# A fused graph-attention, linear-attention and expert layer on one core: the scatter of each expert slot's result is moved behind the slot's own values

## The chip, the core and the metric

The kernel runs on one core of a Trainium2 chip. A core has TensorE (PE in the profile, with its weight loads as PEld), VectorE (DVE), ScalarE (ACT), GpSimd (POOL) and SyncE (SP), which here only issues transfers, and 16 DMA engines which they share. The engines run on their own and wait for each other through semaphores. The metric is the time of one execution on the device, in microseconds (us), as the median of several runs.

## What is computed

```python
xn = _layernorm(x)                                  # x: 384 tokens x 1024
x = x + gnn(xn, edges) + mix(xn)                    # graph attention and linear attention
x = x + ffn(_layernorm(x))                          # the experts

def ffn(xt):                                        # 32 experts, each 1024 x 512 and 512 x 1024
    gates = sigmoid(xt @ expert_sel.T)
    sel_val, sel_idx = top_k(gates, 4)              # four experts for each token
    gate_full = zeros.at[arange(N)[:, None], sel_idx].set(sel_val)
    scores = relu(einsum('nd,edf->nef', xt, keys)) * gate_full[:, :, None]
    return einsum('nef,efv->nv', scores, values)
```

All data are float32. The change touches only the last line's stage, the experts.

## The kernel before

The first 474 us of the profiled execution are the two attention branches and the routing. The rest is the expert stage, which is computed in **slots**. A slot is a batch of 128 lanes (64 tokens for each of two experts, side by side); there are 16 such whole slots, 0 to 15, for the 32 experts, and behind them at least one shared slot of four experts with 32 lanes each, which takes the tokens that did not fit. Its experts are the four whose weights are still in memory from slots 14 and 15; with this input one shared slot runs.

For one slot s the work is, in the order of its data:

- `gather` (POOL, L716): an indirect transfer fetches the rows of the slot's 128 tokens into the one buffer `etmp`. It is issued when the transposes of the slot before have read the buffer.
- `x_T(s)` (PE, L1668): eight transposes of these rows into two banks of the matmul memory (PSUM); ACT (L877) and DVE (L1272) copy one half each to `xgT`.
- `do_keys(s)` (PE, L1585): 32 matmuls, two experts side by side on two halves of the array, into bank 0. ACT (L884) applies relu and gate into `hsb`.
- `h_T(s)` (PE, L1676): four transposes of `hsb` into bank 1; ACT (L888) copies them to `hT`.
- `do_values(s, v)` for v = 0, 1 (PE, L1585): 16 matmuls each, into banks 4 and 5. ACT (L894, `y_hi`) takes the rounded high part `yh`, then DVE (L1279, `y_lo`) the remainder `yl`.
- `put_block(s)` (PE, L1625 and L1626): the scatter. A one-hot matrix `place` (DVE, L1275) times `yh` and `yl` puts the lanes back to the 384 tokens: six puts g = 0 to 5 of two matmuls each, g = 0 to 2 for the columns of v = 0 and g = 3 to 5 for those of v = 1, into banks 6, 7, 4, 5, 6, 7.
- `y_add(s, g)` (DVE, L1284): six additions into the accumulator `acc`.

The waits inside `put_block` matter here: put 0 waits for `yl` of v = 0, put 3 for `yl` of v = 1, and puts 4 and 5, which use banks 6 and 7 for the second time, wait for the additions of puts 0 and 1 of the same slot. Nothing sets the order but the program text: each engine runs its own list, written out by hand. On PE one pass for slot s is `do_keys(s+1)`, `put_block(s-1)`, `x_T(s+2)`, `h_T(s+1)`, `do_values(s)`; so a slot's scatter stands behind the keys of the slot after next. Only the end differs: `put_block(14)` stands directly between the values of slot 14 and those of slot 15, since there are no further keys there.

The weights come from HBM in chunks of 1 MB, eight for a slot (four of keys, four of values), into a ring of 18 places. SP issues a chunk when PE has used up the pair of chunks that held its place before (semaphore `s_spent`, L578 for the middle slots, L623 for keys of slot 15 and values of slots 14 and 15).

Of the kernel before, what the change touches and what calls it, by code (L numbers as in the profile page):

```python
# [37 lines left out]
WHOLE = NE // 2  # L38
# [72 lines left out]
def gps_layer_kernel(nc, x, edges, etw, W, cols, rows, selT, keys, values, C, xt_dram, out):  # L111
# [3 lines left out]
    with ctx:  # L115
# [107 lines left out]
        biv_b = at("biv_b", [P, D], F32, BIV)  # L223

        call = sb("c_all", [P, sum(w for _, w in CONSTS_AT)], F32)
        cst, width = {}, 0
        for n, w in CONSTS_AT:
# [318 lines left out]
        def keys_at(s):  # L546
            return 8 * s - 4 if s >= 2 else 8 * s

        def values_at(s):
            return 8 * s + 8 if s == 1 or 2 <= s < WHOLE - 1 else 4 if s == 0 else 8 * WHOLE - 4  # L550
# [386 lines left out]
        def _(dve):  # L937
# [332 lines left out]
            def x_evict(s, p):  # L1270
                dve.wait_ge(s_xT, s)
                nc.vector.tensor_copy(xgT[p][:, 4:8, :], x_halves[1]).then_inc(s_xd, 1)  # L1272

            def place_of(s, p):
                nc.vector.tensor_scalar(place[p][:, :], iota[:, :], tokf[:, bass.ds(s, 1)], None, ALU.is_equal).then_inc(s_place, 1)  # L1275

            def y_lo(s, v):
                dve.wait_ge(s_yh, 2 * s + v + 1)
                nc.vector.tensor_tensor(yl[:, v, :], ps[4 + v], yh[:, v, :].bitcast(F32), ALU.subtract).then_inc(s_yl, 1)  # L1279

            def y_add(s, g, bank):
                dve.wait_ge(s_put, 6 * s + g + 1)
                rows_of = acc[:, g % NT, g // NT * HALF:(g // NT + 1) * HALF]
                nc.vector.tensor_tensor(rows_of, ps[bank], rows_of, ALU.add).then_inc(s_add, 1)  # L1284

            def dve_slot(s, p, x_ahead=True):
                for g in range(6):
                    y_add(s - 1, g, put_banks[g])
                if x_ahead:
                    x_evict(s + 2, p)  # L1290
                place_of(s, p)
                for v in range(2):
                    y_lo(s, v)
# [4 lines left out]
            y_lo(0, 0)  # L1298
            x_evict(1, 1)
            y_lo(0, 1)  # L1300
            x_evict(2, 0)
            dve_slot(1, 1)
            with dve.Fori(1, WHOLE // 2 - 1) as j:
                for p in range(2):
                    dve_slot(2 * j + p, p)
            dve_slot(WHOLE - 2, 0)
            dve_slot(WHOLE - 1, 0, x_ahead=False)
            turns = dve.value_load(slots[0:1, 0:1], min_val=1, max_val=TURNS_MAX)
# [12 lines left out]
        def _(pe):  # L1321
# [55 lines left out]
            for name in order:  # L1377
# [52 lines left out]
                elif name == "o1":  # L1430

                    for b in range(NT):
                        bs = slice(b * P, (b + 1) * P)
                        for q in range(4):
                            s = j["sub"] + q
# [10 lines left out]
                else:  # L1446
                    xh, xl = src_of[base]
                    for q in range(4):
                        s = j["sub"] + q
# [109 lines left out]
            def token_table():  # L1559

                for q in range(NT * TOPK):
                    if q % TOPK == 0:
                        pe.wait_ge(s_1s, q // TOPK + 1)
                        pe.wait_ge(s_1h, q // TOPK + 1)
                    last = nc.tensor.matmul(ps[5][:, 0:SLOTS], lane1h_h[:, q, :], slot1h_h[:, q // TOPK, q % TOPK, :],
                                            start=(q == 0), stop=(q == NT * TOPK - 1))
                last.then_inc(s_r, 1)
# [11 lines left out]
            def two_experts(c, to, what, k, kc, first, fin):  # L1579

                for side in range(2):
                    half = slice(LANES * side, LANES * side + LANES)
                    if kc == 0:
                        pe.wait_ge(s_ring[at_place[c + side]], ring_landed(c + side, 0))
                    last = nc.tensor.matmul(to[half, :], what[:, k, half], ring[at_place[c + side]][:, kc, :], start=first, stop=fin)  # L1585
                if kc == 3:
                    last.then_inc(s_spent, 1)
# [29 lines left out]
            def put(s, g, p, bank):  # L1617

                v, t = g // NT, g % NT
                if g == 0:  # L1620
                    pe.wait_ge(s_place, s + 1)
                if t == 0:
                    pe.wait_ge(s_yl, 2 * s + v + 1)
                to = place[p][:, t * P:(t + 1) * P]
                nc.tensor.matmul(ps[bank], to, yh[:, v, :], start=True, stop=False)  # L1625
                nc.tensor.matmul(ps[bank], to, yl[:, v, :], start=False, stop=True).then_inc(s_put, 1)  # L1626

            def put_block(s, p, where=put_banks):

                for g in range(6):  # L1630
                    if g in (0, 1) and (not isinstance(s, int) or s >= 1):
                        pe.wait_ge(s_add, 6 * s - 1 + g)
                    if g >= 4:
                        pe.wait_ge(s_add, 6 * s - 3 + g)
                    put(s, g, p, where[g])

            def do_keys(s, p):

                if isinstance(s, int) and s == 0:
                    pe.wait_ge(s_xa, 1)  # L1640
                else:
                    pe.wait_ge(s_xa, s + 2)
                    pe.wait_ge(s_h, s)
                for k in range(DC):
                    if k == DC // 2:
                        if isinstance(s, int) and s == 0:
                            pe.wait_ge(s_xa, 2)
                        else:
                            pe.wait_ge(s_xd, s)
                    if k == TABLE_AT and isinstance(s, int) and s == 0:  # L1650
                        token_table()
                    two_experts(keys_at(s) + 2 * (k // 4), ps[0], xgT[p], k, k % 4, k == 0, k == DC - 1)

            def do_values(s, p, v):
                if v == 0:
                    pe.wait_ge(s_he, s + 1)
                if not isinstance(s, int) or s >= 1:
                    pe.wait_ge(s_add, 6 * s - 3 + v)
                for k in range(EF):
                    two_experts(values_at(s) + 2 * v, ps[4 + v], hT[p], k, k, k == 0, k == EF - 1)  # L1660

            def x_T(s, p, landed):
                pe.wait_ge(s_g[p], landed)
                pe.wait_ge(s_xa, s + 1)
                if not isinstance(s, int) or s >= 2:
                    pe.wait_ge(s_xd, s - 1)
                for b in range(DC):
                    last = nc.tensor.transpose(ps[2 + b // 4][:, (b % 4) * P:(b % 4 + 1) * P], xg[:, b * P:(b + 1) * P], ident[:, :])  # L1668
                last.then_inc(s_xT, 1)

            def h_T(s):
                pe.wait_ge(s_h, s + 1)
                if not isinstance(s, int) or s >= 1:
                    pe.wait_ge(s_he, s)
                for b in range(EF):
                    last = nc.tensor.transpose(ps[1][:, b * P:(b + 1) * P], hsb[:, b * P:(b + 1) * P], ident[:, :])  # L1676
                last.then_inc(s_hT, 1)

            def pe_slot(s, p):

                do_keys(s + 1, 1 - p)
                put_block(s - 1, 1 - p)
                x_T(s + 2, p, 16 * ((s + 3) // 2))
                h_T(s + 1)
                for v in range(2):
                    do_values(s, p, v)

            do_keys(0, 0)
            gate_table()
# [1 line left out]
            do_values(0, 0, 0)  # L1691
            x_T(1, 1, 16)
            do_values(0, 0, 1)
            do_keys(1, 1)
            x_T(2, 0, 16)
            h_T(1)
            for s in range(1, WHOLE - 1):
                pe_slot(s, s % 2)
            put_block(WHOLE - 2, 0)
            for v in range(2):  # L1700
                do_values(WHOLE - 1, 1, v)
            pe.wait_ge(s_slots, 1)
# [57 lines left out]
```

## Time and profile before

| | |
|---|---|
| median of 3 runs | 804.27 us (804.12 to 805.77) |
| the profiled execution | 806.2 us, its span 804.4 us |
| mean granted TensorE clock | 0.998 of full speed |
| busy: PE / PEld / DVE / ACT / POOL | 779.8 / 546.2 / 401.2 / 245.5 / 200.6 us |
| transferred | 207.10 MB, 257 GB/s over the span |
| chain that ended last | PE 79%, SP's queue 6%, DMA 5%, DVE 5% |

The profile cuts the span into 40 slices. From the 26th on (502 us) the rate of the transfers stands at 422 to 427 GB/s in each slice until the 38th (764 us), and the DMA engines are busy without a gap. The busy digit of PE stands at 9 in the same slices, and at 8 in the last of them. Two resources are thus full at once in the expert stage, and the share of busy time alone does not say which of them sets the end.

### The profile page before, as it was taken

The numbers are of one execution on the slowest core, as the hardware profiler recorded it, in microseconds if no ns is written. First come the engines' busy times: TensorE is split into PE (matmuls) and PEld (weight loads), VectorE is DVE, ScalarE is ACT, GpSimd is POOL, SyncE is SP. The second block draws the span as 40 slices with busy tenths as digits, with TensorE's granted clock in tenths as the row PEclk, the third lists the DMA queues.
The fourth block names the chain that finished last, engine by engine and source line by source line (L and its number), as shares of the span: only waits on it lengthen the run. The fifth ranks groups of instructions, "written<-read, shape, count | busy, mean of one in ns | idle before, by whom it ended". The sixth has DMA issues, their size and how long they took to land.

```text
span 804.4 us, 11580 instructions
## 1 busy us (share of the span) xinstructions
PE 779.8 (97%) x4187; PEld 546.2 (68%) x4187; DVE 401.2 (50%) x892; ACT 245.5 (31%) x426; POOL 200.6 (25%) x213
## 2 busy tenths in 40 slices
PE   6999999999999999999999999999999999999897
PEld 6997889988998999997557754444444444444333
DVE  6579976753443346436873784232233323322234
ACT  4453421342332234337882231211111211111101
POOL 2027434544534440006890001100000010000000
PEclk9999999999999999999999999999999999999999
DMA  8962534243343434431107889999999999999936
GB/s 341 404 238 84 204 140 158 59 145 112 115 149 105 143 120 170 151 105 53 53 2 282 346 348 377 425 425 422 427 425 426 426 425 426 425 426 425 424 116 252
DMA packets 35606, 207.10 MB, mean 257 GB/s; under 512 B 7812, under 2 KB 8196, under 8 KB 12256
## 3 DMA queue, kind: packets, MB, share of 16 engines
q1 hardware_dynamic: 27504, 190.85, 59.5%
q0 software_dynamic: 7184, 14.71, 4.9%
q10 hardware_dynamic: 864, 0.83, 0.3%
q8 instruction: 33, 0.54, 0.3%
q14 instruction: 21, 0.17, 0.1%
HBM read 204.91 MB, written 4.43 MB: 260 GB/s over the span
## 4 chain that ended last, share of the span: by engine, by line
PE 79%; SPq 6%; DMA 5%; DVE 5%; issue 2%; ACT 1%; POOL 1%; DVEq 0%; POOLq 0%; ACTq 0%
PE ps L1585 20%; PE ps L1324 14%; PE ps L1326 14%; PE ps L1325 14%; SPq L578 5%; DMA raw<-in_keys 3%; PE ps L1625 2%; PE ps L1626 2%; PE ps L493 2%; PE ps L1597 2%; PE ps L1668 1%; PE ps L482 1%; PE ps L467 1%; DMA etmp<-xt_dram,gidx 1%; SPq L623 1%
## 5 line engine op out<-in xcount | busy, mean ns | idle before, releaser
L965 DVE TENSOR_TENSOR wl<-raw,wh 128x1024 fp32r<-128x1024 f32 x88 | 108.3, 1235 | 118.3 <-ACT wh L771 117.7
L771 ACT ACTIVATE wh<-raw 128x1024 fp32r<-128x1024 f32 x88 | 93.0, 1060 | 193.6 <-PE ps L1326 192.5
L698 POOL DMA_INDIRECT plane<-code,idx x96 | 101.9, 1061 | 120.7 <-DMA plane<-code,idx 95.4
L1284 DVE TENSOR_TENSOR acc<-ps,acc 128x512 f32<-128x512 f32 x102 | 62.5, 681 | 102.8 <-PE ps L1626 102.8
L1585 PE MATMUL ps<-ring,xgT 128*64 128x512 f32 x376 | 100.8, 593 | 3.4 <-DMA ring<-in_keys 3.4
L1585 PE MATMUL ps<-ring,hT 128*64 128x512 f32 x424 | 103.4, 596 | 0.7 <-ACT hT L888 0.7
L1324 PE MATMUL ps<-xnh,wh 128*128 128x384 f32 x256 | 86.9, 340 | 0.9 <-DVE xnl L1059 0.9
L1326 PE MATMUL ps<-xnh,wl 128*128 128x384 f32 x256 | 86.5, 338 | 0.0
L1325 PE MATMUL ps<-xnl,wh 128*128 128x384 f32 x256 | 86.5, 338 | 0.0
L1279 DVE TENSOR_TENSOR yl<-ps,yh 128x512 fp32r<-128x512 f32 x34 | 23.5, 691 | 99.8 <-ACT yh L894 99.8
L1585 PEld LDWEIGHTS ps<-ring,xgT 128*64 128x64 f32 x376 | 31.4, 137 | 58.6 <-issue 52.4
L1585 PEld LDWEIGHTS ps<-ring,hT 128*64 128x64 f32 x424 | 32.4, 137 | 54.0 <-issue 52.2
L456 POOL TENSOR_SCALAR pr<-pr,mx 128x384 f32<-128x384 f32 x40 | 49.4, 1253 | 69.6 <-DVE mx L419 69.6
L714 POOL COPY gcol<-gidx 128x1 int32 (+1 forms) x16 | 2.9, 183 | 244.1 <-PE ps L1668 244.1
L894 ACT ACTIVATE yh<-ps 128x512 fp32r<-128x512 f32 x34 | 20.3, 598 | 103.0 <-PE ps L1585 97.1
L1324 PEld LDWEIGHTS ps<-xnh,wh 128*128 128x128 f32 x256 | 48.1, 188 | 1.3 <-DVE xnl L1059 1.2
L1585 PE MATMUL ps<-raw,xgT 128*64 128x512 f32 x136 | 47.5, 595 | 1.4 <-DMA raw<-in_keys 1.2
L1325 PEld LDWEIGHTS ps<-xnl,wh 128*128 128x128 f32 x256 | 48.1, 188 | 0.1
L1326 PEld LDWEIGHTS ps<-xnh,wl 128*128 128x128 f32 x256 | 48.1, 188 | 0.0
L884 ACT ACTIVATE hsb<-ps,tabf 128x512 f32<-128x512 f32 x16 | 11.0, 689 | 110.4 <-PE ps L1585 103.8
L1625 PE MATMUL ps<-yh,place 128*128 128x512 f32 x102 | 42.4, 416 | 0.0
L1626 PE MATMUL ps<-yl,place 128*128 128x512 f32 x102 | 40.1, 393 | 0.0
(258 smaller groups left out, 1396.6 us busy)
## 6 DMA issues: line engine op xcount, KB each, us to landing
ring<-in_values SPq DMA_DIRECT2D x53, 1024.0 KB, 23.3
ring<-in_keys SPq DMA_DIRECT2D x49, 1024.0 KB, 21.8
raw<-in_keys SPq DMA_DIRECT2D x19, 1024.0 KB, 18.1
raw<-in_values SPq DMA_DIRECT2D x11, 1024.0 KB, 25.7
raw<-in_w_v SPq DMA_DIRECT2D x8, 1024.0 KB, 4.9
raw<-in_w_q SPq DMA_DIRECT2D x8, 1024.0 KB, 4.8
raw<-in_w_k SPq DMA_DIRECT2D x8, 1024.0 KB, 4.8
key_rows<-key_dram POOLq DMA_DIRECT2D x6, 1024.0 KB, 5.8
```

The lines of the kernel that those rows point to most:

```text
L456: nc.gpsimd.tensor_scalar(pr[:, u % RING, :], pr[:, u % RING, :], mx[:, 3, u:u + 1], None, ALU.mult).then_inc(s_p, 1)
L578: sp.dma_start(ring[at_place[n]], src_ap[bass.ds(e[side], 1), half].rearrange("a p k n -> p (a k) n"))\
L698: nc.gpsimd.indirect_dma_start(plane[m], bass.IndirectOffsetOnAxis(idx[:, g:g + 1].bitcast(U32), 0), code[:, g:g + 1], None, bounds_check= ...
L771: nc.scalar.activation(wh[:, s % SUB], raw[:, c % RAW, 2 * (s % 2):2 * (s % 2) + 2, :], ACT.Copy)\
L965: nc.vector.tensor_tensor(wl[:, s % SUB], raw[:, (s // 2) % RAW, 2 * (s % 2):2 * (s % 2) + 2, :], wh[:, s % SUB].bitcast(F32), ALU.subtrac ...
L1284: nc.vector.tensor_tensor(rows_of, ps[bank], rows_of, ALU.add).then_inc(s_add, 1)
L1324: nc.tensor.matmul(o, ah, bh_, start=start, stop=False)
L1325: nc.tensor.matmul(o, ah, bl_, start=False, stop=False)
L1326: return nc.tensor.matmul(o, al, bh_, start=False, stop=stop)
L1585: last = nc.tensor.matmul(to[half, :], what[:, k, half], ring[at_place[c + side]][:, kc, :], start=first, stop=fin)
L1625: nc.tensor.matmul(ps[bank], to, yh[:, v, :], start=True, stop=False)
L1626: nc.tensor.matmul(ps[bank], to, yl[:, v, :], start=False, stop=True).then_inc(s_put, 1)
```

## The change

PE's program is written in another order: `put_block(s)` follows directly on `do_values(s)`, for all slots 0 to 13 (for slot 14 it already does), in place of standing behind `do_keys(s+2)`. On DVE the copy of the rows for slot 2 (`x_evict(2, 0)`) moves behind the six additions of slot 0. ACT, POOL and SP have the instructions that they had, in the same order, and no instruction is added or removed.

```diff
@@ vector @@
             def dve_slot(s, p, x_ahead=True):
                 for g in range(6):
                     y_add(s - 1, g, put_banks[g])
+                if isinstance(s, int) and s == 1:
+                    x_evict(2, 0)
                 if x_ahead:
                     x_evict(s + 2, p)
...
             y_lo(0, 1)
-            x_evict(2, 0)
             dve_slot(1, 1)
@@ tensor @@
             def pe_slot(s, p):
                 do_keys(s + 1, 1 - p)
-                put_block(s - 1, 1 - p)
                 x_T(s + 2, p, 16 * ((s + 3) // 2))
                 h_T(s + 1)
                 for v in range(2):
                     do_values(s, p, v)
+                put_block(s, p)
...
             do_values(0, 0, 1)
+            put_block(0, 0)
             do_keys(1, 1)
             x_T(2, 0, 16)
             h_T(1)
             for s in range(1, WHOLE - 1):
                 pe_slot(s, s % 2)
-            put_block(WHOLE - 2, 0)
             for v in range(2):
                 do_values(WHOLE - 1, 1, v)
```

On PE at slot 1, before. The `xgT0` rows are keys of slot 2, `yh_97,place0_99` with `yl` the scatter of slot 0, `etmp` and `hsb` the transposes `x_T(3)` and `h_T(2)`, `hT1` the values of slot 1, and `ring2_79,xgT1_94` the first keys of slot 3:

```order
L1585 MATMUL ps<-ring15_90,xgT0_93 64x512
L1625 MATMUL ps<-yh_97,place0_99 128x512
L1626 MATMUL ps<-yl_98,place0_99 128x512
...
L1668 MATMUL ps<-c_all,etmp 128x128 x8
L1676 MATMUL ps<-c_all,hsb_101 128x128 x4
L1585 MATMUL ps<-ring16_91,hT1_96 64x512
...
L1585 MATMUL ps<-raw_76,hT1_96 64x512 x8
L1585 MATMUL ps<-ring2_79,xgT1_94 64x512
```

The same stretch after the change (line numbers are one higher):

```order
L1586 MATMUL ps<-ring15_90,xgT0_93 64x512
L1669 MATMUL ps<-c_all,etmp 128x128 x8
L1677 MATMUL ps<-c_all,hsb_101 128x128 x4
L1586 MATMUL ps<-ring16_91,hT1_96 64x512
...
L1586 MATMUL ps<-raw_76,hT1_96 64x512 x8
L1626 MATMUL ps<-yh_97,place1_100 128x512
L1627 MATMUL ps<-yl_98,place1_100 128x512
...
L1586 MATMUL ps<-ring2_79,xgT1_94 64x512
```

The twelve matmuls of a scatter have gone from between the keys and the transposes, and those of the slot's own result (`place1`, slot 1) stand between its values and the next keys.

On DVE at the first slots, as a difference. `xgT_93` is the copy of the rows for slot 2, `xgT_94` that for slot 1 and then for slot 3:

```order
 L1279 TENSOR_TENSOR yl<-ps,yh 128x512
+L1284 TENSOR_TENSOR acc<-ps,acc 128x512 x6
 L1272 COPY xgT_93<-ps 128x512
-L1284 TENSOR_TENSOR acc<-ps,acc 128x512 x6
 L1272 COPY xgT_94<-ps 128x512
```

The six additions of slot 0 now come ahead of the copy for slot 2, as their puts do on PE.

## Rows read from the trace of the kernel before

**Rows 1.** Windows: length, busy us by engine, granted clock, DMA share, GB/s

```profile
547.38:565.54 18.16, 18.16 (x91) 8.03 (x89) 5.99 (x10) 2.97 (x5) 1.25 (x2) 1.00 1.01 423
...
768.00:780.00 12.00, 12.00 (x68) 4.04 (x71) 5.52 (x10) 1.19 (x2) 0.00 (x0) 1.00 0.05 20
```

**Rows 2.** Waits of PE after 503 us: waiter, releaser, us in total, times, longest

```profile
PE ps L1585 <- DMA ring<-in_keys: 3.4, 3, 1.3
...
PE ps L1585 <- DMA raw<-in_keys: 1.2, 1, 1.2
```

**Rows 3.** Chain that ended last, from 700 us: start, length, what

```profile
723.90 27.96 DMA raw<-in_keys
751.90 3.65 PE ps L1585 x14
```

**Rows 4.** Timeline of PE: last keys, scatter, transposes, values, as in every slot

```profile
546.86 0.59 PE L1585 MATMUL ps<-ring,xgT 128*64 128x512 f32 x1
547.38 0.50 PE L1625 MATMUL ps<-yh,place 128*128 128x512 f32 x1
...
550.25 1.03 PE L1668 MATMUL ps<-c_all,etmp 128*128 128x128 f32 x8
551.12 0.60 PE L1676 MATMUL ps<-c_all,hsb 128*128 128x128 f32 x4
551.65 0.65 PE L1585 MATMUL ps<-ring,hT 128*64 128x512 f32 x2
```

**Rows 5.** Timeline of PE, then ACT, where no scatter stands between keys and transposes

```profile
501.76 0.59 PE L1585 MATMUL ps<-raw,xgT 128*64 128x512 f32 x1
502.28 1.09 PE L1668 MATMUL ps<-c_all,etmp 128*128 128x128 f32 x8
503.21 0.64 PE L1676 MATMUL ps<-c_all,hsb 128*128 128x128 f32 x4
...
502.46 0.69 ACT L884 ACTIVATE hsb<-ps,tabf 128x512 f32<-128x512 f32 x1 [6.33 <-PE ps L1585]
```

**Rows 6.** Timeline of PE, ACT, DVE: scatter of slot 14, directly behind its values

```profile
765.82 1.03 PE L1585 MATMUL ps<-ring,hT 128*64 128x512 f32 x4
766.78 0.50 PE L1625 MATMUL ps<-yh,place 128*128 128x512 f32 x1
...
768.27 0.50 PE L1625 MATMUL ps<-yh,place 128*128 128x512 f32 x1
...
769.81 0.40 PE L1626 MATMUL ps<-yl,place 128*128 128x512 f32 x1
770.13 1.08 PE L1585 MATMUL ps<-ring,hT 128*64 128x512 f32 x4
...
766.90 0.60 ACT L894 ACTIVATE yh<-ps 128x512 fp32r<-128x512 f32 x1 [2.84 <-PE ps L1585]
...
767.53 0.69 DVE L1279 TENSOR_TENSOR yl<-ps,yh 128x512 fp32r<-128x512 f32 x1 [2.75 <-ACT yh L894]
768.14 3.67 DVE L1284 TENSOR_TENSOR acc<-ps,acc 128x512 f32<-128x512 f32 x6
```

**Rows 7.** Two gathers on L716: start, and us from issue to landing

```profile
L716 POOL DMA_INDIRECT etmp<-xt_dram,gcol x1: 1043/1043/1043, 493.2 to 493.2; - x1
...
DMA to landing us min/median/max: 4.9/4.9/4.9
...
L716 POOL DMA_INDIRECT etmp<-xt_dram,gcol x1: 1017/1017/1017, 504.7 to 504.7; - x1
...
DMA to landing us min/median/max: 8.9/8.9/8.9
```

**Rows 8.** Timeline of PE: first transpose of the rows of slot 3

```profile
513.93 1.04 PE L1668 MATMUL ps<-c_all,etmp 128*128 128x128 f32 x8
```

**Rows 9.** L623, two of the value chunks: duration and start of issues, us to landing

```profile
L623 SPq DMA_DIRECT2D ring<-in_values x2: 333/3595/6857, 733.1 to 733.7; - x2
DMA to landing us min/median/max: 28.5/29.4/30.3
```

## The prediction

> **What bounds the kernel now.** I read the page first, for the stage: from 502 us to 764 us both PE and the DMA engines are full. Busy shares can't rank them, so the next view is the windows. A middle slot takes 18.16 us with PE busy for all of it while the transfers run at 423 GB/s [rows 1]. A slot's eight chunks and its gather are 8.4 + 0.5 = 8.9 MB, which at that rate take about 21 us. PE uses weights faster than they arrive; it lives on the ring, which was full when the stage began. The waits show when that store runs out: after 503 us PE waits for weights four times, 3.4 + 1.2 = 4.6 us in all [rows 2], and all of it late, in the keys of slots 13, 14 and 15 (the rows do not name the slots; their place follows from the last wait, below, one slot of about 21 us apart). The last wait ends at 751.90 us, where the chain that ended last goes over from a transfer of 27.96 us to PE [rows 3]. Behind it nothing more is waited for from HBM, and from 768 to 780 us PE is full with the DMA engines at 0.05 [rows 1]. So the end is set by the weights, **but only by 4.6 us**: had PE needed 4.6 us more of its own before 751.9 us, those waits would be gone and the end would be where it is. What the change is worth depends on how much PE time it adds, against that reserve.
>
> **What the change does to PE in one slot.** The same twelve matmuls run, so only the joints between pieces differ.
>
> Where the scatter is taken out: before, from the last keys pair to the first values matmul it is 551.65 - 546.86 = 4.79 us [rows 4]. After, it is keys, `x_T`, `h_T`, values. The trace has that sequence once, since slot 1's keys have no scatter behind them: last pair to `x_T` 502.28 - 501.76 = 0.52 us, `x_T` to `h_T` 503.21 - 502.28 = 0.93 us [rows 5]. The latter has a new wait in it: `h_T` needs `hsb`, which ACT finishes at 502.46 + 0.69 = 503.15 us [rows 5]; the scatter used to cover that. It is small, since eight transposes without a wait take 551.12 - 550.25 = 0.87 us [rows 4]. From `h_T` to values 0.53 us [rows 4]; `hT` of that slot is a slot old by then, so nothing waits. Sum 0.52 + 0.93 + 0.53 = 1.98 us, against 4.79: **2.81 us less**.
>
> Where it is put in: the trace has this once too, at slot 14 [rows 6]. The first put starts at 766.78, the next work at 770.13: 3.35 us. The same block in the middle takes 550.25 - 547.38 = 2.87 us [rows 4]. The chain inside is plain: values end, `yh` at 766.90 for 0.60 us, `yl` at 767.53 for 0.69 us, and put 3, which needs this `yl`, starts at 768.27. The first six matmuls just about cover it. Then DVE's additions, 3.67 / 6 = 0.61 us each from 768.14 us, pace puts 4 and 5, because banks 6 and 7 must be read before they are written again. Before the change the additions were paced by PE, now PE by the additions. To that comes the joint from values to scatter: the last group of values is two pairs of matmuls from 765.82 on, 1.03 us with the 0.59 of one matmul [rows 4], so pairs follow each other after some 0.43 us; the last pair starts at 766.25 and the put 0.53 us later, where the next keys pair would follow after 0.43 us: 0.10 us. Put in: 3.35 + 0.10 = **3.45 us more**.
>
> Net 3.45 - 2.81 = **0.64 us for each moved scatter**. Fourteen are moved (slots 0 to 13): 14 x 0.64 = 9.0 us. The row that could be too pessimistic is the last joint, 770.13 - 769.81 = 0.32 us from the last put matmul to the values [rows 6], where a put matmul in the middle of the stage takes 2.87 / 12 = 0.24; it might be a wait for an addition that keys don't have. Without it the term is 14 x 0.54 = 7.6 us. I take 8.7, near the measured pair, and keep 7.6 and 9.0 as ends. Queued behind the waiting puts on PE are the next keys, and behind them SP's issues, which wait for used chunks; those come later by the same time.
>
> **The gather of slot 3.** In the prologue keys 1 and keys 2 follow each other with no values between, so the two `x_T` there lie closest. Before, `x_T(2)` starts at 502.28 and `x_T(3)` at 513.93 [rows 5, 8], with the scatter of slot 0 between; the gather for slot 3 is issued at 504.7 and lands 8.9 us later, at 513.6 [rows 7], 0.3 us ahead of need. Now the scatter of slot 0 stands ahead of keys 1: `x_T(2)` and the gather's issue move by 3.45 us, to 505.7 and 508.1; `x_T(3)` would be ready at 513.93 + 3.45 - 2.87 = 514.5. With 8.9 us the gather lands at 517.0 and PE waits 2.5 us; with the 4.9 us of the gather before it [rows 7] it lands at 513.0 and nothing waits. The four chunks queued ahead of it are the same, but the engines have had 3.4 us more to work on them, so I take the middle, 6.9 us: a wait of **0.5 us**, with 0 and 2.5 as ends. All later `x_T` have values and a scatter between them, over 18 us apart, and don't wait.
>
> What the rows show here is that a gather lands late when weights are queued (8.9 against 4.9 us). The Trainium skill, DMA: Bandwidth & Descriptors, section "Queues, rings and completion order", says that each DMA engine goes round the queues that have work, a packet at a time, so weights queued by SP should not delay a gather on POOL's queue by their number. By that rule the gather would land after about 4.9 us whatever is queued and the term would be 0; the trace speaks against it.
>
> **The starvation of the transfers.** Chunks freed by keys 1 and 2 are released 3.45 us later, at a time when the DMA queue is short. This could shift the whole stream by up to 3.45 us. I cost it at nothing, and the cover is the same as the reserve turned round: at the last weight wait (751.90 us) PE would now arrive at 751.9 - 4.6 + 8.7 + 0.5 + 2.81 = 759.3 us (the 2.81 because the scatter of slot 13 is done by then and its gap not yet recovered), 7.4 us after the chunk has landed. If the stream shifts by 3.45 us it is still 4 us early.
>
> **Sum.** PE's own time grows by 8.7 + 0.5 = 9.2 us; the 4.6 us of weight waits go, since PE is now late for all of them. +4.6 us. On the profiled execution, 806.2 + 4.6 = 810.8 us; it lies 1.9 us over the median, so on the median 804.27 + 4.6 = **808.9 us**. The stretch from slot 15's values to the end holds no moved instruction and no weight wait, so all of it is passed on.
>
> **Rivals.**
> *The weights still bind, and the time falls.* If the scatter costs behind its values what it costs elsewhere (2.87 us, the wait of slot 14 being special to it), a slot gains only 0.16 us, 2.2 us in all, under 4.6. Then the transfers set the end as before, and PE, after the chunk of 751.90, has no scatter of slot 13 left: up to 2.81 us less, cut by the second chunk of the second half of slot 14's values, which lands at 733.1 + 28.5 = 761.6 us [rows 9]. Those eight pairs of 0.43 us end at 766.25 + 0.43 = 766.7 [rows 6], so they began at 763.2, and 1.6 us can be won: 802.7 us. The sign turns at 0.33 us a slot (14 x 0.33 = 4.6). Against it: [rows 6] has the same buffers, banks and operations as every other slot. 8%.
> *No change to be measured.* A cost of about 0.3 to 0.45 us a slot, between the two: 803 to 805.9 us. 7%.
> *The gather lands late*, with its full 8.9 us: 804.27 + 9.0 + 2.5 - 4.6 = 811.2 us. For it: it is the nearest gather by place and load. 17%.
> *The additions cost more*: if they fall behind further, with the put waits growing to one addition of 0.61 us more a slot for half of the slots, +4.3: 813.2 us. Nothing in [rows 6] shows it. 6%.
> *The skill's round robin*: no gather wait, 804.27 + 8.7 - 4.6 = 808.4 us; it is inside the forecast.
>
> **How the numbers follow.** Forecast 808.9 us, 62%, its own range 807.2 (7.6 and no gather wait) to 810. Rivals 8, 7, 17 and 6%. The range holds forecast and late gather and reaches a little to either side: 806.0 to 812.0 us. About 0.2% (1.6 us) is what a measurement of this kernel can tell from no change: faster 8%, within 7%, slower 85%.
>
> **What would show it.** In the profile of the changed kernel: a middle slot of 18.8 us in place of 18.16; the scatter 3.3 to 3.4 us long, with put 3 directly behind the end of `yl`; `h_T` 0.93 us behind `x_T`; the weight waits in keys of slots 13 to 15 gone; one wait of `x_T(3)` for its gather of 0 to 2.5 us; chunks of slot 15's keys landed some 7 us ahead of use. The prediction is wrong if a middle slot stays under 18.5 us, or if PE still waits for weights near 750 us.

## The result

The changed kernel takes **812.62 us** (median of three runs, 810.62 to 812.75) against 804.27 us: it is slower, by a ratio of 1.0076 (95% interval 1.005 to 1.0101). That ratio is the recorded comparison of the runs; the two medians of three alone lie 8.35 us apart, which is more (1.0104). The forecast, 808.9 us, has the right sign and the right mechanism and is too low; the median lies 0.6 us over the upper end of the range. A second set gave 811.59 us (4 runs) against 805.66 us (19 runs), 5.9 us apart, again a ratio of 1.0076 (1.006 to 1.0093). So the change costs about 6 us by the ratio and by the larger set, where 4.6 were forecast.

First, what the forecast named as its signs. The page of the changed kernel, the parts that correspond to the table before: the span, PE's busy time, and the chain that ended last by engine.

```profile
span 810.9 us, 11580 instructions
...
PE 790.5 (97%) x4187; PEld 539.3 (67%) x4187; DVE 401.6 (50%) x892; ACT 245.7 (30%) x426; POOL 197.6 (24%) x213
...
PE 89%; DVE 5%; DMA 2%; issue 1%; ACT 1%; POOL 1%; DVEq 0%; SPq 0%; POOLq 0%; ACTq 0%
```

SP's queue and nearly all transfers have gone from the chain (6% and 5% before): in the expert stage PE sets the end, no longer the weights. The timeline of PE for one whole slot of the changed kernel, from the scatter of slot 2 to that of slot 3, which corresponds to [rows 4] (start, length, instruction; the keys between are left out):

```profile
546.47 0.50 PE L1626 MATMUL ps<-yh,place 128*128 128x512 f32 x1
...
547.97 0.49 PE L1626 MATMUL ps<-yh,place 128*128 128x512 f32 x1
...
549.82 0.64 PE L1586 MATMUL ps<-ring,xgT 128*64 128x512 f32 x1
...
556.83 1.09 PE L1669 MATMUL ps<-c_all,etmp 128*128 128x128 f32 x8
557.78 0.66 PE L1677 MATMUL ps<-c_all,hsb 128*128 128x128 f32 x4
558.37 7.09 PE L1586 MATMUL ps<-ring,hT 128*64 128x512 f32 x32
565.39 0.50 PE L1626 MATMUL ps<-yh,place 128*128 128x512 f32 x1
```

A slot takes 565.39 - 546.47 = 18.92 us in place of 18.16. The scatter takes 549.82 - 546.47 = 3.35 us, to the hundredth what [rows 6] had for slot 14, and put 3 stands 1.50 us behind put 0. ACT and DVE in the same scatter show why:

```profile
546.58 0.60 ACT L894 ACTIVATE yh<-ps 128x512 fp32r<-128x512 f32 x1 [2.75 <-PE ps L1586]
...
547.21 0.69 DVE L1279 TENSOR_TENSOR yl<-ps,yh 128x512 fp32r<-128x512 f32 x1 [2.66 <-ACT yh L894]
547.82 2.47 DVE L1284 TENSOR_TENSOR acc<-ps,acc 128x512 f32<-128x512 f32 x4
```

`yl` ends at 547.90, and put 3 starts at 547.97. The wait of the third slot's transposes for their gather is there too (first row: PE; then the gather on POOL and its landing):

```profile
519.06 1.09 PE L1669 MATMUL ps<-c_all,etmp 128*128 128x128 f32 x8 [1.72 <-DMA etmp<-xt_dram,gcol]
```

```profile
L716 POOL DMA_INDIRECT etmp<-xt_dram,gcol x1: 1017/1017/1017, 510.9 to 510.9; - x1
...
DMA to landing us min/median/max: 8.2/8.2/8.2
```

And the waits for weights. The prediction read them from the matmuls [rows 2]. The same view for the weight **loads** (PEld) after 503 us, the kernel before first (engine, line, releaser: us in total, times, longest), then the changed one:

```profile
PEld ps L1585 <- DMA ring<-in_keys: 6.0, 3, 2.2
PEld ps L1585 <- DMA raw<-in_keys: 2.7, 2, 2.1
PEld ps L1625 <- DVE acc L1284: 1.2, 4, 0.3
PEld ps L1625 <- DVE yl L1279: 0.6, 2, 0.3
```

```profile
PEld ps L1626 <- DVE acc L1284: 9.0, 30, 0.3
PEld ps L1626 <- DVE yl L1279: 4.0, 15, 0.3
PEld ps L1669 <- DMA etmp<-xt_dram,gcol: 2.6, 1, 2.6
```

The waits for HBM's weights, 8.7 us, are gone, and in their place stand fifteen waits for `yl` and thirty for additions: two puts in each of fifteen scatters. (The waits of loads can't simply be added up as a cost, since a load may wait while the matmul before it still runs: for the gather of slot 3 the load waited 2.6 us and PE lost 1.8.)

### The profile page after: what moved, and what is told of

Its sections match the earlier page's. It is cut to its first block, busy times and chain, and to the rows that moved or that the text cites. A ratio compares the mean times of both kernels' runs of the same rounds, so it can differ in the third digit from the quotient of the medians.

```text
span 810.9 us, 11580 instructions
## 1 busy us (share of the span) xinstructions
PE 790.5 (97%) x4187; PEld 539.3 (67%) x4187; DVE 401.6 (50%) x892; ACT 245.7 (30%) x426; POOL 197.6 (24%) x213
## 4 chain that ended last, share of the span: by engine, by line
PE 89%; DVE 5%; DMA 2%; issue 1%; ACT 1%; POOL 1%; DVEq 0%; SPq 0%; POOLq 0%; ACTq 0%
PE ps L1586 27%; PE ps L1325 14%; PE ps L1327 14%; PE ps L1326 14%; PE ps L1626 4%; PE ps L1627 3%; PE ps L1669 2%; PE ps L493 2%; PE ps L1598 2%; PE ps L482 1%; PE ps L467 1%; PE ps L1677 1%; DMA etmp<-xt_dram,gcol 1%; DVE wl L965 1%; PE ps L1533 1%
## 5 line engine op out<-in xcount | busy, mean ns | idle before, releaser
L698 POOL DMA_INDIRECT plane<-code,idx x96 | 99.4, 1036 | 119.2 <-DMA plane<-code,idx 92.0
L1586 PE MATMUL ps<-ring,hT 128*64 128x512 f32 x424 | 105.8, 609 | 0.7 <-ACT hT L888 0.7
L1272 DVE COPY xgT<-ps 128x512 f32<-128x512 f32 x17 | 11.7, 690 | 100.6 <-PE ps L1669 100.6
L1626 PE MATMUL ps<-yh,place 128*128 128x512 f32 x102 | 46.9, 460 | 0.0
```

The costliest lines, as they stand in the source:

```text
L698: nc.gpsimd.indirect_dma_start(plane[m], bass.IndirectOffsetOnAxis(idx[:, g:g + 1].bitcast(U32), 0), code[:, g:g + 1], None, bounds_check= ...
```

## Where 6 us come from

The profiled executions enter the expert stage at different times, from 474.40 to 481.00 us, in code that the change doesn't touch. So stretches are compared, each from the rows of its own trace: from the first keys matmul of slot 0, and from the first transpose of `x_T(1)`, which is the last thing ahead of the moved instructions, to the end of the span.

| kernel | first keys | x_T(1) | span | keys to end | x_T(1) to end |
|---|---|---|---|---|---|
| before | 474.57 | 490.80 | 804.4 | 329.8 | 313.6 |
| before, again | 479.42 | 495.93 | 809.4 | 330.0 | 313.5 |
| changed | 475.37 | 493.50 | 810.9 | 335.5 | 317.4 |
| changed, again | 474.87 | 492.37 | 809.8 | 334.9 | 317.4 |
| pad_small | 474.90 | 493.04 | 805.1 | 330.2 | 312.1 |
| pad_large | 476.13 | 492.52 | 808.7 | 332.6 | 316.2 |
| before_late | 474.46 | 491.25 | 804.9 | 330.4 | 313.6 |
| after_late | 474.60 | 491.01 | 810.6 | 336.0 | 319.6 |
| put0_late | 474.41 | 490.67 | 805.7 | 331.3 | 315.0 |
| other_banks | 481.00 | 497.86 | 812.2 | 331.2 | 314.3 |
| split | 474.55 | 492.11 | 803.3 | 328.8 | 311.2 |
| last_only | 476.05 | 492.86 | 803.4 | 327.3 | 310.5 |
| last_only, again | 474.40 | 490.96 | 802.4 | 328.0 | 311.4 |

Two profiles of the kernel before agree within 0.1 us from `x_T(1)` on, and so do two of the changed kernel: the moved instructions cost 317.4 - 313.55 = **3.8 us**. (The two of last_only differ by 0.9 us.) The rest, 1.0 to 1.9 us, lies ahead of `x_T(1)`: 18.1 and 17.5 us from the first keys in the changed kernel's two profiles, 16.2 and 16.5 in those of before. Nothing there was moved. From the first keys to the end the difference is 4.9 to 5.7 us. In the first profile of the changed kernel PE ran at half the granted clock (1.2 in place of 2.4 GHz) around 490 us, with its values at 6.20 us for what takes 3.65 (columns of the windows as in [rows 1]; then the row of PE):

```profile
484.00:488.00 4.00, 3.31 (x23) 2.58 (x24) 3.93 (x4) 0.60 (x1) 0.26 (x1) 0.71 0.95 363
488.00:492.00 4.00, 4.00 (x12) 1.18 (x10) 1.94 (x5) 0.00 (x0) 0.00 (x0) 0.50 0.96 383
```

```profile
487.37 6.20 PE L1586 MATMUL ps<-ring,hT 128*64 128x512 f32 x16 [0.69 <-ACT hT L888]
```

In the second profile the clock was full and the first gather landed late. Both happen in kernels whose code up to there is the same (the half clock in pad_small and other_banks, the late gather in split, 17.6 us from the first keys), and after_late, which has the moved order, has neither (16.4 us). So they are taken as no part of the change. Whether a kernel *pays* for them is, as the experiments show.

## The experiments

The theory that the profiles suggest: (1) the reserve of PE against the weights (the PE time that can be added before the end moves) was 8.3 to 8.7 us, not 4.6; (2) that reserve also took up late starts in the prologue, and the change has spent it. The rival to each is named in the expectations. "Before" in each set is the kernel before on the same chip: 805.66 us for the first four kernels, 806.01 for the next four, 806.21 for the last three.

**The changed kernel once more.**

> The changed kernel unchanged, for its spread. Its three timed runs were 810.62, 812.62 and 812.75 us, and the profiled one (812.75) had a stretch at half the granted clock from 485 to 493 us, before the first moved instruction, that cost about 2.8 us. Theory A (that stretch is chance, and the change itself is worth about +6 us): the times fall in two groups, near 810.5 without it and near 812.7 with it, and the mean clock tells them apart. Theory B (the stretch belongs to the changed program): every profile of it has the stretch, and none of the kernel before.

Measured: 811.59 us (810.94 to 812.85), and the profile has a mean clock of 1.000. So the half clock does not belong to the changed program, as theory A says. But the two groups that it expected did not show: this profile took 811.58 us, 1 us over the 810.5 expected, and a run of the first set took 812.62 us at a mean clock of 0.997. The half clock is not all that separates the runs: without it the first gather was 1.3 us later than in the profile of before.

**How large is the reserve?** Two kernels with a known amount of PE work added to the kernel before, by running transposes twice:

```diff
-                h_T(s + 1)
+                h_T(s + 1, 2 if s <= WHOLE - 3 else 1)     # pad_small
...
-                x_T(s + 2, p, 16 * ((s + 3) // 2))
+                x_T(s + 2, p, 16 * ((s + 3) // 2), 2 if s <= WHOLE - 3 else 1)     # pad_large
```

> The kernel before, with the four transposes h_T run twice in slots 1 to 13 (same data, same result): 0.44 us more of TensorE in each slot, 13 x 0.44 = 5.7 us ahead of the last weight wait. The reserve of TensorE against the weights is 4.6 us by the waits of matmuls (the prediction's number) and 8.3 to 8.7 us by the waits of the weight loads and by the slot lengths. With 4.6 the kernel is 1.1 us slower than before; with 8.3 it is within 0.3 us of it.

> The kernel before, with the eight transposes x_T run twice in slots 1 to 13: 0.87 us more of TensorE in each slot, 13 x 0.87 = 11.3 us. Reserve 4.6 us: +6.7 us. Reserve 8.3 us: +3.0 us, and no wait of TensorE for weights is left.

pad_small: 806.47 us, a ratio of 1.0003 (0.999 to 1.0016), for 5.6 us of added work. pad_large: 809.60 us, 1.0049 (1.0032 to 1.0065), 3.9 us more for 11.3 us of work. A reserve of 4.6 us would have given 1.1 and 6.7 us. The timed runs of pad_small can't tell 1.1 us from none (their interval reaches to 1.3 us); those of pad_large rule 6.7 us out (2.6 to 5.2 us) and by themselves put the reserve at some 6 to 9 us. By the stretch from the first keys to the end the two are 0.2 to 0.4 and 2.6 to 2.8 us over before, so the profile of pad_large puts the reserve at 11.3 - 2.7 = 8.6 us. In its trace, as expected, the weight loads wait for nothing from HBM after 503 us; pad_small has one such wait left:

```profile
PEld ps L1585 <- DMA raw<-in_keys: 1.2, 1, 1.2
```

**Does the reserve take up a late prologue?** One edit in both kernels: the transposes of `x_T(1)` are run four times, so PE is 2.6 us later, once.

```diff
-            x_T(1, 1, 16)
+            x_T(1, 1, 16, 4)
```

> The kernel before, with the eight transposes x_T(1) in the prologue run four times (same data, same result): TensorE gets to everything behind them 2.6 us later, once. Theory A (the end hangs on the weights, and the reserve takes up what delays TensorE in the prologue): within 0.8 us of the kernel before, and the waits for weights near the end, 8.7 us for the weight loads, come down to about 6. Theory B (every delay is passed on): +2.6 us, the waits at the end unchanged.

> The changed kernel with the same four-fold x_T(1). It has no waits for weights left, so by both theories the 2.6 us are passed on: 2.6 us slower than the changed kernel, about 8.5 us slower than before. Together with the run above this tells what a late first gather or a stretch at half the clock costs in the one kernel and in the other.

From `x_T(1)` to the end the kernel before takes 313.6 us with the delay and 313.55 without it: nothing of 2.6 us arrives. (From the first keys, 0.4 to 0.6 us does.) In the changed kernel it is 319.6 against 317.4: 2.2 us do. The timed runs say less. before_late has 807.48 us, 1.0016 (1.0001 to 1.0031): 1.3 us over before, more than the 0.8 us of theory A, while the 2.6 us of theory B (1.0032) lie just outside the interval. after_late has 813.62 us, 1.0103 (1.0086 to 1.012), where the changed kernel alone had 1.0076: 2.2 us. The waits of before_late for weights fell as the theory wants, from 8.7 to 5.1 us:

```profile
PEld ps L1585 <- DMA ring<-in_keys: 2.9, 2, 2.2
PEld ps L1585 <- DMA raw<-in_keys: 2.2, 2, 1.6
```

So by the profiles theory B falls for the kernel before, and the timed runs lean the same way. A second profile of the kernel before bounds this:

> The kernel before, unchanged, for a second profile beside the others. Theory A (the end of the kernel before hangs on the weights): if TensorE enters the expert stage later or has a stretch at half the clock there, the waits for weights near 710 to 750 us shrink by that much and the end moves by less. Theory B (TensorE sets it): the distance from the first keys of slot 0 to the end is the same within 0.3 us plus such a stretch.

Its one time is 811.29 us. It entered the stage 4.85 us later and ended 5.0 us later, with the waits for weights hardly changed (8.9 us for keys, 0.3 for values). Here theory B described it: a delay *ahead of the first keys* moves the weights too, because SP is held up by PE there. In both profiles SP waits, between 455 and 500 us, the same 7.4 us for the work just ahead of the first keys (L1532), and then 13.8 us for the first keys and values:

```profile
SPq L605 <- PE ps L1585: 13.8, 3, 6.8
...
SPq L605 <- PE ps L1532: 7.4, 1, 7.4
```

The reserve takes up only what comes behind the first keys.

**The gather.**

```diff
             do_values(0, 0, 1)
-            put_block(0, 0)
             do_keys(1, 1)
...
                 do_keys(s + 1, 1 - p)
+                if s == 1:
+                    put_block(0, 0)
```

> The changed kernel with the scatter of slot 0 (and DVE's copy for slot 2) back in its old place behind the keys of slot 2; slots 1 to 13 stay as changed. If the wait of x_T(3) for its gather comes from the scatter of slot 0 standing ahead of keys 1, the wait of 1.8 us goes, and with it 0.76 us of joints: 2.5 us faster than the changed kernel, 3.4 us slower than before. If the gather is late for another reason, only 0.8 us is gained.

DVE's copy for slot 2 goes back with it. 809.19 us (1.0046, 1.0026 to 1.0067), 2.4 us better than the changed kernel's 811.59 us of the other set, and 315.0 us from `x_T(1)` on, where the changed kernel takes 317.4. The wait is gone: `x_T(3)` and its neighbours read as in [rows 8], and the slots after it still take 18.92 us.

```profile
513.84 1.04 PE L1668 MATMUL ps<-c_all,etmp 128*128 128x128 f32 x8
```

**What in the scatter costs?** First the banks; the waits that guard their reuse are changed to match.

```diff
-        put_banks, end_banks = (6, 7, 4, 5, 6, 7), (6, 7, 0, 1, 6, 7)
+        put_banks, end_banks = (6, 7, 1, 4, 5, 6), (6, 7, 0, 1, 6, 7)
```

> The changed kernel with the scatter's banks 6, 7, 4, 5, 6, 7 replaced by 6, 7, 1, 4, 5, 6, so that put 4 waits for no addition of its own slot and put 5 only for the first. If additions pace puts 4 and 5, a scatter behind its values takes 3.0 us in place of 3.35 and a slot 18.6 in place of 18.92 us: 14 x 0.3 = 4.5 us less, about 1.5 us slower than before or the same. If the loss is in the wait for yl alone, nothing changes.

PE in one scatter of it, puts 0, 3, 4 and the keys that follow:

```profile
569.06 0.50 PE L1626 MATMUL ps<-yh,place 128*128 128x512 f32 x1
...
570.56 0.50 PE L1626 MATMUL ps<-yh,place 128*128 128x512 f32 x1
...
571.13 0.40 PE L1626 MATMUL ps<-yh,place 128*128 128x512 f32 x1
...
572.15 2.37 PE L1586 MATMUL ps<-raw,xgT 128*64 128x512 f32 x10
```

The scatter takes 3.09 us in place of 3.35 and a slot 18.65 in place of 18.92; puts 4 and 5 no longer wait, put 3 still stands 1.50 us behind put 0. From `x_T(1)` on it is 3.1 us shorter than the changed kernel (14 x 0.27 would be 3.8). The timed runs don't show it: 812.6 us, 1.0057 (1.0029 to 1.0084), from 806.96 to 815.0 in two groups, where 1.5 us over before or less was expected. This kernel entered the stage late in its profile, at 481.0 us, in unchanged code, and for most of its runs that may hold as well, which is not shown. So the pacing by additions is shown by the trace, at 0.27 us a slot, and the end-to-end gain is inconclusive.

```diff
                 do_keys(s + 1, 1 - p)
-                put_block(s - 1, 1 - p)
+                put_block(s - 1, 1 - p, puts=range(3, 6))
...
                     do_values(s, p, v)
+                put_block(s, p, puts=range(3))
```

> The kernel before with half of each scatter moved, for slots 0 to 13: puts 0 to 2, whose input is ready by then, stand behind the slot's values, puts 3 to 5 stay behind the keys of the slot after next. If the change loses by the wait of put 3 for yl and of puts 4 and 5 for additions, a slot here stays within 0.1 us of 18.16 (0.1 for a joint more), the weights still set the end, and the three puts no longer ahead of slot 14's values give 1.4 us: 1 to 1.5 us faster than before. If it loses by the joints themselves, a slot is 0.5 us longer and the kernel slower than before.

Neither number was met. A slot takes 18.53 us, 0.37 more than before, although no put waits; the changed kernel's is 0.76. The first half scatter, puts 0 to 2 with no wait in them, and the first keys behind it:

```profile
542.98 0.50 PE L1625 MATMUL ps<-yh,place 128*128 128x512 f32 x1
543.32 0.39 PE L1626 MATMUL ps<-yl,place 128*128 128x512 f32 x1
543.55 0.40 PE L1625 MATMUL ps<-yh,place 128*128 128x512 f32 x1
...
544.57 0.64 PE L1585 MATMUL ps<-ring,xgT 128*64 128x512 f32 x1
```

Six matmuls of 0.23 us each would be 1.39 us; the block takes 1.59, because the step from the first matmul to the second is 0.34 us and that into the keys 0.33. The step into the block is 0.09 us longer than that from values into keys before, and the keys take 7.01 in place of 6.97 us. The other half of the scatter, which stands ahead of the transposes as before, has the longer first step too (0.34 us), but the step into the transposes is 0.23. So one block more in a slot costs 0.1 us at each of three places, its entry, its first step and its exit into keys, without any wait, and a little in the keys. It is still not slower than before: 805.18 us, 0.9988 (0.9967 to 1.0009), and 1.1 us less from the first keys to the end. 13 x 0.37 = 4.8 us of PE are taken up by the reserve, and the three puts missing behind the last weights come off the end.

**Only the last scatter.** If a scatter moved to where PE waits anyway is free, one fewer behind the last weights is a gain.

```diff
                 do_keys(s + 1, 1 - p)
-                put_block(s - 1, 1 - p)
+                if s < WHOLE - 2:
+                    put_block(s - 1, 1 - p)
...
                     do_values(s, p, v)
+                if s == WHOLE - 3:
+                    put_block(s, p)
```

> The kernel before with one scatter moved, that of slot 13, to directly behind the values of slot 13; the others stay behind the keys. If the weights set the end of the kernel before and leave 8.3 us of reserve, the 3.45 us put in lie in time in which TensorE waits for weights anyway, and the 2.81 us taken out behind the last keys come off the end, cut by the landing of slot 14's values: 1.6 to 2.8 us faster than before. If TensorE's own work sets the end, it is 0.7 us slower.

> The kernel before with only the scatter of slot 13 moved behind its values, a second time and with more rounds, since the first gave 0.999 (0.9981 to 1.0). If the 2.8 us that the distance from slot 15's first transposes to the end became shorter are real, the median is 1 to 2.5 us under before; if the weights' arrival varies by as much from run to run, it is within 0.5 us.

804.87 us against 805.66 (0.999, 0.9981 to 1.0), which is 0.8 us where 1.6 to 2.8 were expected, and with more rounds 804.21 against 806.01 (0.998, 0.9965 to 0.9995), 1.8 us, within the 1 to 2.5 expected then. From the first keys to the end the two profiles take 327.3 and 328.0 us, against 329.8 and 330.0: 2.2 us less in the mean. PE in the first of them, at the place that in the kernel before held the wait that ended at 751.90 [rows 3]:

```profile
750.48 4.08 PE L1585 MATMUL ps<-ring,xgT 128*64 128x512 f32 x17
757.50 1.09 PE L1668 MATMUL ps<-c_all,etmp 128*128 128x128 f32 x8
```

From the first keys matmul of slot 15 to `x_T(16)` it is 7.02 us, keys alone, with no wait. The scatter of slot 13 has filled the two waits for the weights of slot 15; those of slots 13 and 14 are still there (4.6 us for the loads). This version beats the changed kernel clearly and the kernel before narrowly: the first interval reaches to no gain, the second to 0.05%.

## Why the prediction was right, and where its terms were wrong

*What bounds the kernel.* Right in kind: the weights set the end by a few microseconds only, and the change spends more PE time than that. The step that failed is "after 503 us PE waits for weights four times, 3.4 + 1.2 = 4.6 us". That is what the waits of the matmuls show; the weight loads waited 8.7 us. The wait at 709.55 us shows how the two differ. The last `ring` matmul ahead of it starts at 706.86 us, but the `raw` ones of the other half run on to 708.30 us by their modelled end, and only from there does the matmul's row count its 1.24 us. The load counts 2.12 us, and that slot was 2.30 us longer (20.46 us from one `x_T` to the next, in place of 18.16). Another wait, 0.57 us at 725.02 us, is in the loads' rows alone. The rows at 709.55 us, two of matmuls and one of the load:

```profile
706.97 1.33 PE L1585 MATMUL ps<-raw,xgT 128*64 128x512 f32 x3
709.55 0.64 PE L1585 MATMUL ps<-ring,xgT 128*64 128x512 f32 x1 [1.24 <-DMA ring<-in_keys]
...
709.55 0.13 PEld L1585 LDWEIGHTS ps<-ring,xgT 128*64 128x64 f32 x1 [2.12 <-DMA ring<-in_keys]
```

Rows that could have told it stood in the same trace: thirteen slots from `x_T(3)` [rows 8] to `x_T(16)`, the row below, take 758.36 - 513.93 = 244.4 us, and 13 x 18.16 is 236.1. The difference, 8.3 us, is the reserve. pad_large confirms it, and pad_small agrees.

```profile
758.36 1.04 PE L1668 MATMUL ps<-c_all,etmp 128*128 128x128 f32 x8
```

*The cost in a slot.* 0.62 us were taken (8.7 / 14), 0.76 measured. The scatter (3.35), its chain through `yh` and `yl`, and `h_T` 0.95 us behind `x_T` came as read from [rows 5, 6]. The whole of a slot adds up: scatter 3.35 in place of 2.87 us, `x_T` to `h_T` 0.95 in place of 0.87, `h_T` to values 0.59 in place of 0.53, values 7.02 in place of 6.92, keys 7.01 in place of 6.97; 0.76 us together. The prediction's own 0.64 lacked the 0.06 behind `h_T`, 0.04 in the keys and 0.02 in `h_T`'s wait. Of the scatter's 0.48 us, 0.10 are the step into the keys, so only some 0.38 are waits for `yl` and additions. With the 0.08 ahead of `h_T` the waits come to 0.46 us, and the other 0.30 are joints in which nothing waits. The lower end, 0.54, on the ground that the last joint of 0.32 us might be a wait for an addition, was wrong: split shows that joint, 0.33 us, where nothing is waited for. Fourteen slots: 10.6 us in place of 8.7.

*The gather of slot 3.* The mechanism was right, the middle between two rows was not, and there was no ground for it but that it was the middle: it landed 8.2 us after its issue, and PE lost 519.06 - (510.25 + 7.02) = 1.8 us in place of 0.5. In both profiles of the changed kernel the gathers from this one on take 6.8 to 9.1 us, 8.3 in the median; only the one before it takes 4.2 and 5.8. The weights' own time from issue to landing tells how long SP's queue is. In the profile of the changed kernel its median is 8.4 us at 500 to 520 us and 27.5 at 700 to 720, while the gathers issued at 510.9 and 710.6 us take 8.2 and 9.1. The Trainium skill (DMA: Bandwidth & Descriptors, "Queues, rings and completion order") says that each DMA engine takes turns between the queues that have work, a packet at a time. The trace agrees in that the number of queued weights hardly matters, 8.2 against 9.1 us. What the prediction drew from the rule, that a gather beside queued weights would land after 4.9 us as the first one did, does not follow from taking turns, and 8.2 us were measured.

*The starvation of the transfers* cost nothing, as said: no load waits for weights in the changed kernel. The stream did shift. The chunk that in the kernel before landed at 751.90 us, 277.3 us behind the first keys, is issued at 726.3 us here and lands 28.5 us later, 279.4 us behind them; its first matmul starts at 761.46 us, so it lies there for 6.7 us, near the 7 that were forecast.

*The sum.* By the trace 10.6 + 1.8 - 8.6 = 3.8 us from `x_T(1)` on. The forecast was 4.6: three terms were off, and the reserve, 4.0 us too small, hid the other two, 3.2 us too small together. With the right reserve and the other terms as they stood the forecast would have been 8.7 + 0.5 - 8.6 = 0.6 us, no change; so its nearness to the trace is partly luck. That the time moved by 6 us and not 3.8 fits what was not in the sum at all: the kernel before takes up late gathers and clock dips in the prologue, the changed one pays them, 1.0 to 1.9 us in each of its two profiles against those of before. That the average run has as much is not shown, only that the two profiles had it and that such a delay is passed on.

*The rivals.* That the weights still bind and the time falls did not come true for the change, but it is what last_only does, and split in its profile (its timed runs, 0.9967 to 1.0009, show no clear gain). "The additions cost more" is refuted (18.92 or 18.93 us for every slot from the third on). The late gather was nearer than the forecast's 0.5 us: 1.8 of its 2.5 us came.

## What to carry to other kernels

When two resources are both full, find out how much later the second could have been, and find it from the distance between the same instruction in successive iterations, not from the matmuls' own waits; here that would have given 8.3 us in place of 4.6. A producer placed directly ahead of its consumer on an engine that runs its list in order costs that part of the chain between them which no other work covers. Here that was part of the wait for evict and subtract and the additions that free the banks, some 0.38 us a slot, and 0.30 more came from joints in which nothing waits. Where the engine would have waited anyway the move is free: move only those instances. And a reserve that a change spends was also protecting the kernel from delays that a single profile may not show.

## What the runs showed of the hardware

Three things that were not expected. A block of scatter matmuls between values and keys costs about 0.1 us each at its entry, its first step and its exit, with no wait: the steps are 0.34 us at the start and 0.33 into the keys where the block's inner ones are 0.23. Into the transposes it is 0.23 us too, so the exit depends on what follows.

An indirect gather of 128 rows took 8.0 to 9.1 us from issue to landing through most of the stage, while the weights beside it went from 8.4 to 27.5 us.

And the granted clock can fall to half in one execution and stay full in the next of the same program. Around 490 us it did so in one of two profiles of the changed kernel and in pad_small, for some 7 us each, and for some 3 us in other_banks; in the other ten profiles it stayed full. In the changed kernel it had fallen by 485.64 us, where `h_T` took 1.05 us in place of 0.64. What sets it off is open: PE's idle time of 0.69 us ahead of the values stands in the profiles with a full clock as well.
